# A new order of blocks in a fused attention and FFN kernel whose five engine programs are written by hand

## The reference

```python
w = weight[adapter_ids]                       # condition: one 512x512 matrix per batch
c = jnp.einsum('bsi,boi->bso', x, w)
q, k, v = c @ Wq, c @ Wk, c @ Wv              # 32 heads of 16, 8 groups of k and v
q, k = _apply_rope(q, cos_t, sin_t), _apply_rope(k, cos_t, sin_t)
scores = jnp.where(causal, -jnp.inf, qg @ k^T)
x = x + (softmax(scores / sqrt(16)) @ v) @ Wo
y = x @ W^T + ((x @ lora_A[labeler]) @ lora_B^T) * 0.5
base = y @ W_base^T + b_base
top2 experts of (y @ W_router^T), softmax over the two, one rank-16 update each
x = x + base + lora
```

## Time and profile before

| | |
|---|---|
| runs (us) | 246.0, 246.1, 247.74; median 246.1 |
| span of the profiled execution | 244.0 us, 2.1 below the median of the runs; it counts from the first instruction to the last |
| PE busy | 230.3 us, 94% of the span |
| DVE, ACT, POOL busy | 182.1 (75%), 121.5 (50%), 96.9 (40%) |
| chain that ended last | PE 74%, DVE 15%, issue 3%, ACT 3%, DMA 2% |
| moved by DMA | 21.18 MB, mean 87 GB/s |

### The profile page before, as it was taken

The page is one execution under the profiler, slowest core; times in us unless marked ns, Lnnn a source line. Parts: engine busy times, 40 slices in busy tenths (PEclk is TensorE's granted clock), DMA queues, the critical chain, the costliest instruction groups (busy, mean ns, idle before and its releaser), DMA issues.

```text
span 244.0 us, 5779 instructions
## 1 busy us (share of the span) xinstructions
PE 230.3 (94%) x2010; PEld 175.3 (72%) x2010; DVE 182.1 (75%) x903; ACT 121.5 (50%) x271; POOL 96.9 (40%) x108
## 2 busy tenths in 40 slices
PE   6899998989899999999999999999999998999893
PEld 6688975766578677867777777777777774556793
DVE  2789357538966996699659965997599769949663
ACT  3687435577276256716671667166712660254010
POOL 7300572468269125912592249224932320002120
PEclk9999999999999999999999999999999999999999
DMA  5999308015002610161016101710100110003011
GB/s 134 339 378 349 151 6 266 1 18 201 12 3 50 212 51 6 43 218 45 11 47 215 45 13 46 215 45 13 43 3 25 33 43 3 0 3 89 10 46 43
DMA packets 20049, 21.18 MB, mean 87 GB/s; under 512 B 6452, under 2 KB 11572, under 8 KB 20020
## 3 DMA queue, kind: packets, MB, share of 16 engines
q1 hardware_dynamic: 20020, 20.81, 27.0%
HBM read 18.71 MB, written 2.10 MB: 85 GB/s over the span
## 4 chain that ended last, share of the span: by engine, by line
PE 74%; DVE 15%; issue 3%; ACT 3%; DMA 2%; SPq 1%; POOL 1%; DVEq 0%; ACTq 0%
PE bank L1030 12%; PE bank L1035 11%; PE bank L1031 10%; PE bank L1091 5%; PE bank L1118 5%; DVE thrown L725 5%; PE bank L1041 4%; PE bank L1057 4%; PE bank L1132 3%; PE bank L1134 3%; PE bank L1133 3%; PE bank L1084 2%; DMA stage_d<-base_t 2%; PE bank L1098 2%; PE bank L1267 2%
## 5 line engine op out<-in xcount | busy, mean ns | idle before, releaser
L725 DVE CUSTOM_DVE_ANT_0 thrown<-bank,causal 128x128 f32<-128x128 f32 x256 | 56.2, 287 | 0.2
L359 POOL TENSOR_TENSOR cond_w_lo<-cond_raw,cond_w_hi 128x512 fp32r<-128x512 f32 x28 | 35.3, 1289 | 22.8 <-ACT cond_w_hi L442 22.8
L379 POOL TENSOR_TENSOR rope_b<-rope_a,rope_b 128x128 f32<-128x128 f32 (+1 forms) x16 | 16.3, 1018 | 38.1 <-DVE rope_b L777 38.1
L442 ACT ACTIVATE max_rows<-bank,own_p 128x128 fp32r<-128x128 f32 x32 | 9.1, 370 | 26.0 <-PE bank L1067 26.0
L388 POOL TENSOR_TENSOR x_bias<-x,bias_row 128x512 f32<-128x512 f32 x8 | 10.2, 1280 | 29.8 <-DVE out_sb L898 28.4
L1030 PE MATMUL bank<-qkv_w_hi,c_t_hi 128*128 128x512 f32 (+1 forms) x64 | 21.3, 350 | 0.6 <-DVE c_t_lo L662 0.5
L725 DVE DVE_READ_ACCUMULATOR2_ANT neg_max<- 128x1 f32 x256 | 21.4, 84 | 0.0
L1030 PE MATMUL bank<-fused_w_hi,late 128*128 128x324 f32 (+2 forms) x68 | 21.2, 325 | 0.0
L1031 PE MATMUL bank<-qkv_w_lo,c_t_hi 128*128 128x512 f32 (+1 forms) x64 | 20.5, 337 | 0.0
L1031 PE MATMUL bank<-fused_w_lo,late 128*128 128x324 f32 (+2 forms) x68 | 19.9, 306 | 0.0
L400 POOL TENSOR_TENSOR out_sb<-stage_b,x_bias 128x324 f32<-128x324 f32 x5 | 4.4, 883 | 37.0 <-ACT stage_b L442 37.0
(11 more groups left out here) (163 smaller groups left out, 642.5 us busy)
## 6 DMA issues: line engine op xcount, KB each, us to landing
cond_raw<-cond_w_t SPq DMA_DIRECT2D x7, 1024.0 KB, 5.6
xt_raw<-x_t SPq DMA_DIRECT2D x8, 256.0 KB, 5.9
x_nat<-x SPq DMA_DIRECT2D x8, 256.0 KB, 2.7
out<-out_sb SPq DMA_DIRECT2D x8, 256.0 KB, 2.2
stage_d<-base_t SPq DMA_DIRECT2D x4, 256.0 KB, 4.5
cond_raw<-cond_w_t SPq DMA_DIRECT2D x4, 256.0 KB, 4.3
stage_b<-w SPq DMA_DIRECT2D x4, 256.0 KB, 5.3
stage_a<-w_q SPq DMA_DIRECT2D x4, 256.0 KB, 5.4
```

What stands on the lines that cost most here:

```text
L359: pool.tensor_tensor(cond_w.lo[:, k, :], cond_raw[:, k, :], f32(cond_w.hi[:, k, :]), ALU.subtract).then_inc(cond_lo, 1)
L379: pool.tensor_tensor(qk[:, at:at + w], rope_a[:, at:at + w], rope_b[:, at:at + w], ALU.add).then_inc(qk_ready, 1)
L442: return nc.scalar.activation(out, in_, ACT.Copy, scale=scale)
L725: nc.vector.tensor_tensor_reduce(thrown[:, p % 2, j, e, :], s_ps[j][:, at:at + P], causal[:, :], -1.0, -MASKED, ALU.add, ALU.min, neg_max[ ...
```

## The change

The same blocks on the same buffers are called in another order on four engines; some blocks are cut in two so that others can go between (`condition` by k, `project_q` and ffn parts into high and low). Three waits are added where an order no longer implies them: `maxima(0,0)` waits for both tables, VectorE's `add_x_base(LAST)` for its bank, and `project_kv_high` of the first two batches for the split of c and of its weights. Because lines are added, line numbers of the changed kernel are larger (L1118 becomes L1186, for instance).

```diff
             tables()
             split_xt(0)
-            for f in range(2):
-                split_condition(f + 1, 0)
-                split_condition(f + 1, 1)
-                add_rotated(f, rope_k, D, KV)
-                add_rotated(f, rope_q, 0, D)
-                split_condition(f + 1, 2)
-                split_condition(f + 1, 3)
-                split_xt(f + 1)
+            split_condition(1, 0)
+            split_xt(1)
+            add_rotated(0, rope_k, D, KV)
+            split_condition(1, 1)
+            add_rotated(0, rope_q, 0, D)
+            split_condition(1, 2)
...
+            for t in range(2, LAST - 1):
+                f, r, q, g = t + 1, t - 1, t - 2, t + 2
+                split_a(r)
+                split_condition(g, 0)
+                split_condition(g, 1)
+                split_condition(g, 2)
+                split_condition(g, 3)
+                add_rotated(f, rope_q, 0, D)
                 add_rotated(f, rope_k, D, KV)
+                add_bias(q)
+                add_x_base(q)
+                split_xt(g)
+                add_out(q)
+            add_bias(4)
+            add_x_base(4)
+            add_out(4)
+            split_a(5)
+            add_rotated(7, rope_q, 0, D)
+            add_rotated(7, rope_k, D, KV)
+            add_bias(LAST - 2)
...
+            for t in range(2, LAST - 2):
                 f, r, q, g = t + 1, t - 1, t - 2, t + 2
+                spread_maxima(t)
+                split_context(r)
+                exp_scores(t, 0)
+                copy_v(f)
+                split_k(f)
+                split_x1(r)
+                split_q(f)
+                exp_scores(t, 1)
+                empty_left(r)
+                exp_top(r)
+                split_a(t)
+                copy_c(g)
+                split_hidden(r)
+                split_c(g)
+                split_condition(t + 3, range(KT))
+                split_xt(t + 3)
+                empty_right(r)
...
-            owns()
             split_rank()
...
             sign_sin()
+            owns()
+            rotate_k(0)
             split_fused(4)
-            rotate_k(0)
             rotate_q(0)
...
+            for t in range(2, LAST - 1):
+                f, r, q, g = t + 1, t - 1, t - 2, t + 2
+                turn_back(r)
+                rotate_q(f)
+                split_context(r)
+                rotate_k(f)
+                add_x(r)
...
+                maxima(f, 3)
+                split_maxima(f)
+                scale_context(t, 1)
...
+            turn_context(LAST - 1, 1)
             split_maxima(LAST)
-            turn_context(LAST - 1, 1)
...
+            split_low(LAST - 1)
             turn_back(LAST)
-            split_low(LAST - 1)
...
             warm_up(16)
             fuse(0)
+            fuse(1)
             condition(0)
-            fuse(1)
+            fuse(2)
             transpose_c(0)
-            fuse(2)
             fuse(3)
             fuse(4)
+            project_kv(0)
             project_q(0)
-            project_kv(0)
...
+            for t in range(2, LAST - 1):
+                f, r, q, g = t + 1, t - 1, t - 2, t + 2
+                condition(f, range(2))
+                condition(f, range(2, KT))
+                ffn_high(q, 1, right_ps(q))
+                transpose_hidden(q)
+                ffn_low_half(q, 1, right_ps(q))
+                ffn_rank(q, 1, right_ps(q))
+                transpose_c(f)
+                score(t, 2)
+                score(t, 3)
+                context(r, 1)
+                project_q_high(f)
+                project_q_low(f)
+                finish_ffn(q)
+                project_kv_high(f)
+                transpose_maxima(t)
+                project_kv_low(f)
+                mask_t(t, 0)
+                passes_t(t, 0)
+                less_maxima(t, 0)
+                project_out(r)
+                mask_t(t, 1)
+                transpose_qk(f)
+                transpose_x1(r)
...
+                score(f, 0)
+                score(f, 1)
+                context(t, 0)
...
+            ffn_high(LAST - 2, 1, right_ps(LAST - 2))
             context(LAST - 1, 0)
-            context(LAST - 1, 1)
+            ffn_low_half(LAST - 2, 1, right_ps(LAST - 2))
             keep_busy(6)
             score(LAST, 2)
             score(LAST, 3)
-            project_ffn(LAST - 2, 1, right_ps(LAST - 2))
+            context(LAST - 1, 1)
             keep_busy(12)
             transpose_maxima(LAST)
...
+            ffn_rank(LAST - 2, 1, right_ps(LAST - 2))
             project_out(LAST - 1)
...
+            ffn_high(LAST - 1, 1, right_ps(LAST - 1))
             project_out(LAST)
+            ffn_low_half(LAST - 1, 1, right_ps(LAST - 1))
             transpose_hidden(LAST - 1)
+            ffn_rank(LAST - 1, 1, right_ps(LAST - 1))
             transpose_x1(LAST)
             finish_ffn(LAST - 1)
             keep_busy(6)
             project_low(LAST)
             project_ffn(LAST, 0, left_ps(LAST), slice(0, GATES)).then_inc(gates_done, 1)
+            ffn_high(LAST, 1, right_ps(LAST))
             project_ffn(LAST, 0, base_ps(LAST), slice(GATES, HALF)).then_inc(base_done, 1)
-            project_ffn(LAST, 1, right_ps(LAST))
+            ffn_low_half(LAST, 1, right_ps(LAST))
             transpose_hidden(LAST)
+            ffn_rank(LAST, 1, right_ps(LAST))
```

More of the change, by code:

```diff
@@ new lines, in _ @@
+            maxima(1, 1)
+            turn_context(0, 0)
+            scale_context(0, 0)
+            split_c(2)
+            maxima(1, 2)
+            turn_context(0, 1)
+            maxima(1, 3)
+            split_maxima(1)
+            scale_context(0, 1)
+            turn_back(0)
+            rotate_q(2)
+            split_context(0)
+            rotate_k(2)
+            add_x(0)
+            split_k(2)
+            split_x1(0)
+            split_q(2)
+            split_low(0)
+            choose_experts(0)
```

415 lines of the change are left out of this document (224 added, 191 removed).

## The result

The changed kernel takes 248.17 us (median of nine runs, 247.8 to 249.37) against 246.1 (245.87 to 247.74): ratio 1.0084, 95% interval 1.0055 to 1.0112. The forecast was 245.8 with 242.7 to 248.2 as the range, so the sign was missed; the time lies at the very top of the range. The profiled execution has a span of 246.2 us, 2.2 more than before. The starts of `score(t,2)` divide these 2.2. Up to `score(6,2)` each stands behind the same work in both kernels.

What follows compares the result with a forecast made beforehand. TensorE's own work was taken to bound the rounds. Opening -0.2, rounds 2 to 5 +1.45, round 6 -0.2 and tail -1.3 sum to -0.25, about 245.8 us against 246.1; range 242.7 to 248.2.

Steps and rivals of the forecast that it cites:

- What bounds the kernel: Rounds: TensorE busy 115.94 of 116 us, so only its own work can gain and every new wait costs fully.
- VectorE's piece from rank to score: From ffn_rank's last matmul to score, 7.89 us: moving add_bias takes off at least 0.52, which gives nothing by itself.
- TensorE's own work: Each round: fewer changes of tile shape on TensorE save 0.39 us, 24.70 to 24.31; bounds 0 and -0.5.
- the context behind the scores: context(t,0) moved behind the scores in each round: saves about one and a half shape changes, 0.15 us.
- The new wait: Rounds 2 to 5: add_x waits for the later add_bias, so TensorE waits 0.75 at transpose_x1; round +0.36, four +1.45.
- the first rival: Rounds: the wait at transpose_x1 doesn't arise; rounds of 24.31, 242.8 us in all; chance 0.20.
- the wait at transpose_maxima: Rounds 2 to 5: transpose_maxima waits some 0.07 us for split_maxima, held by GpSimd's fourth split_condition.
- The chain: Rounds 2 to 5, s being score(t,2)'s start: split_condition, split_maxima, rotate_q, add_rotated, add_bias, add_x; transposes of x at s + 13.5.
- The step that failed in the opening: Opening: earlier fused weights and first maxima against owns beside split_condition; -0.2 us, bounds -0.9 and +1.5.
- The tail: Behind the rounds: idle before batch 6's rank and transpose_x1(7) goes, ffn parts move; -1.3 us, bounds 0 and -2.2.
- The slower one I had named: Rounds: add_rotated q takes the lock ahead of split_context, a wait of 1.55, +1.16 per round; 249.0 us; chance 0.13.

Runs made afterwards that it cites:

- e2: Changed kernel, but in rounds 2 to 5 GpSimd's fourth split_condition stands behind add_x_base instead of ahead of add_rotated; 247.73 us.
- e1: Changed kernel, but in rounds 2 to 5 GpSimd runs add_bias first in its round and add_x_base right behind split_a; 245.95 us.
- e12: As e9, with owns at the start of VectorE's program instead of behind the sign of the sine; 243.14 us.
- e5: Changed kernel, but in the opening ScalarE's split_xt(1) stands behind split_fused(5) and GpSimd's behind split_condition(1,3); 247.34 us.
- e9: Changed kernel with e1 and e5, split_xt(2) behind add_rotated(1), split_experts behind round 2's add_x_base, 20 instead of 12 fillers before transpose_maxima(7); 243.39 us.
- e7: Kernel before with only the changed order of the tail on TensorE and VectorE (everything behind the last round); 245.16 us, in two groups.
- e10: As e7, with 20 instead of 12 filler matmuls before transpose_maxima(7); 244.27 us.

## Why the prediction was wrong, step by step

**What bounds the kernel** was right: every wait that the change put into the rounds cost its full length, and round 4 of e2 shows no gain beyond TensorE's own steps, so what the change took off VectorE's piece from rank to score gave nothing there.

**TensorE's own work** was forecast at -0.39 a round and is about -0.33: round 4 of e2 is 24.73 with 0.36 of wait in it, so 24.37 of work. The parts are there (finish_ffn takes 0.75 to 0.76 from start to start instead of 0.94 to 0.95, transpose_hidden 0.03 instead of 0.16); the context behind the scores takes as long as before (0.99 to 1.00), so it and transpose_hidden together give 0.13 and not the 0.20 forecast.

**The new wait** was the right mechanism, and at transpose_x1 it has the size that was put into the sum: transpose_qk with the idle behind it takes 1.31 instead of 0.60, and transpose_x1 0.59 instead of 0.53 (from start to start, changed kernel and e1), 0.77 together against the 0.75 forecast. That all of it comes from the hold at split_maxima (the first rival's case) was wrong; half does (round 4 of e2), and the whole goes when add_bias is moved (e1).

**The step that failed in the rounds** is the wait at transpose_maxima. I gave it 0.07 and left it out of the sum, since I let it only shift TensorE's arrival. It is 0.15 to 0.2 in rounds 3 and 4 and 0.58 in round 5. The chain itself was right to 0.15 us; what failed is the wait taken from it. Its end, s + 13.5, lies 0.95 behind the arrival without any wait (s + 12.74 less 0.19), and that is the delay of the round; with the 0.07 added to the arrival (s + 12.62, not 12.65) 0.89 would be left at transpose_x1, and I wrote 0.7 to 0.8.

With 0.95 the chain gives a round of 25.26, +0.56, and four rounds +2.24: the sum would then have been 0.54 slower, the right sign, and rounds 3 and 4 measure 25.29 and 25.31.

The rest, in round 5, came over a path that I never followed. I let ScalarE's copies follow at once without asking whether their weights had landed: add_out, moved to the end of GpSimd's round, releases the store that stands ahead of the load in SyncE's program, and with a longer transfer the load landed behind its use instead of 3.7 ahead of it. No run tests this path by itself; e2 shows it again, and in e1, where GpSimd has add_bias off this way, the load of round 5 goes out at s - 7.67 and ScalarE doesn't wait. Rounds 2 to 5 cost +0.50, +0.59, +0.61 and +1.02 instead of 0.36 each.

**The step that failed in the opening** is its sum: -0.2 forecast, +1.31 measured. I looked at `owns` (which costs nothing, e12) and not at the two split_xt. ScalarE's costs about 0.5 in the changed kernel's profile (86.21 against 85.68 in e5, which moves GpSimd's split_xt(1) with it) and up to 1.46 more, at fuse(5), when the transfer lands late; GpSimd's split_xt(2), which holds split_maxima(0), costs about 0.65 (85.68 in e5, 85.03 in e9, which also moves add_bias and split_experts; the idle that it makes is 0.82). With both put back the opening is about as long as before (85.03 in e9 against 84.90).

**The tail** was right in kind and size: -1.82 for round 6 and tail against -1.5, and by itself -1.5 to -2.0 (e7's first group, e10). I booked nothing for the clock, which the new idle can halve; it didn't in the changed kernel's nine runs.

**The rivals.** The slower one I had named didn't happen: split_context came before add_rotated q, as forecast, and its margin held. The slower case that did happen is made of waits I had seen in kind but looked for at other places.

## What to carry to other kernels

When a block is moved on a helper engine, list everything that waits for its semaphore, the transfers above all, and what stands behind them in the queue that issues them: here a store released by the moved block held back a load, and two engines further on TensorE waited. An earlier use needs the same look at what it uses. Where one engine holds up another, as GpSimd and VectorE do here, a new order has to be read as pairs (what of the one runs beside what of the other), and the cheapest place for a block is where its engine is idle and the other does nothing that can be held. A wait that is put into a profile's sum has to stand there once as a delay of the end, and not only as a later arrival at the next wait.

## What the runs showed of the hardware

A VectorE operation of some 0.2 us beside a GpSimd one was held for what was left of it, up to 1.2 us longer than alone (CAST 0.84 and 1.28, TENSOR_TENSOR 1.21 and 1.22, TENSOR_SCALAR 1.42 in the rows above; each ends 0.03 to 0.05 behind the GpSimd operation); for the 128x32 CAST no row of the kernel before had shown it. The Trainium skill, "SBUF — State Buffer", section "Who interferes with whom", states that the two engines share a pair of ports as an exclusive lock, and that whoever comes first has it for a whole instruction while the other is blocked; the rows of CAST and TENSOR_TENSOR agree. In the TENSOR_SCALAR's case VectorE's row begins 0.11 ahead of that of split_experts (81.12), so who came first there the rows don't tell. And an idle of 1.5 us on TensorE was followed, in half of e7's runs, by some 3 us at half the clock (one traced, the others by their mean), worth 1.4 us; in the kernel before, where the longest idle beyond the opening is 1.07, three of 51 runs beside the experiments have a mean clock of 0.989 or 0.990 and are some 1.3 us longer; where their clock fell no trace shows.
